# Four cross-attention and expert layers on one core: dense expert stages run by chunk with the next attention's opening inside, and other orders at the sparse stages

## The reference, cut to what matters

```python
# x: 2048 tokens x 256;  ctx: 1601 context rows x 192;  fp32 throughout
x = x + xattn(layernorm(x), ctx)    # L0: 16 heads of 16
x = x + ffn0(layernorm(x))
x = x + xattn(layernorm(x), ctx)    # L1: 16 heads of 16
x = x + ffn1(layernorm(x))
x = x + xattn(layernorm(x), ctx)    # L2: 8 heads of 32
x = x + ffn2(layernorm(x))
x = x + xattn(layernorm(x), ctx)    # L3: 16 heads of 16
x = x + ffn3(layernorm(x))

xattn:  q = x Wq + bq;  k = ctx Wk + bk;  v = ctx Wv + bv
        softmax(q k^T / sqrt(head)) v  Wo + bo
ffn0:   16 experts 256 -> 128 -> 256 with silu, 4 of 16 by sigmoid scores
        and groups, plus a shared silu layer 256 -> 512 -> 256
ffn1:   top 2 of 8 experts 256 -> 1024 -> 256 with gelu and biases
ffn2:   top 2 of 8 linear experts 256 -> 256 with biases
ffn3:   top 2 of 16 gated experts 256 -> 352 -> 256, at most 320 tokens
        each, plus a shared gated layer of the same size
```

## Time and profile before

| | |
|---|---|
| median of three runs | 3974.86 us (3974.20 to 3976.17) |
| the profiled execution | 3966.67 us |
| its span on the core | 3964.9 us |
| attention 0 and the routing of stage 0 | 0 to 775.0 us |
| dense stage 0, its first to its last matmul | 775.0 to 1069.5 us |
| last matmul of stage 0 to the first score of attention 1 | 78.9 us |
| sparse stage 1, first routed projection | 1827.87 us |
| dense stage 2, its first to its last matmul | 2859.9 to 2973.0 us |
| last matmul of stage 2 to the first score of attention 3 | 76.1 us |
| sparse stage 3, first routed transposes | 3739.41 us |

### The profile page before, as it was taken

How to read it: one execution, slowest core, us unless ns; L and a number is a source line. 1 busy time by engine, 2 the same in 40 slices (tenths; PEclk the granted TensorE clock), 3 DMA queues, 4 the chain that set the end, 5 groups by cost and what they waited for, 6 DMA issues and landing times. The chain is left out here.

```text
span 3964.9 us, 51571 instructions
## 1 busy us (share of the span) xinstructions
PE 3634.5 (92%) x17554; PEld 1586.3 (40%) x17555; DVE 2535.3 (64%) x5339; ACT 1936.7 (49%) x2351; POOL 689.4 (17%) x976
## 2 busy tenths in 40 slices
PE   5999999799889999977998599999797999998997
PEld 2333333456533333324665233332442333332564
DVE  5888887544588888834223555554467888885523
ACT  2677777412237777752333144444203777777111
POOL 4300000300130010014221401010403000001143
PEclk8999999899989999988999699999798999999998
DMA  7100000320010000025002300000411000001134
GB/s 137 41 18 18 14 18 6 68 43 19 15 45 18 17 14 18 9 68 192 30 30 59 100 18 18 17 18 6 86 20 49 18 14 18 17 11 44 40 125 137
DMA packets 132064, 163.82 MB, mean 41 GB/s; under 512 B 38315, under 2 KB 111645, under 8 KB 129681
## 3 DMA queue, kind: packets, MB, share of 16 engines
q1 hardware_dynamic: 121712, 135.08, 12.0%
q0 software_dynamic: 10144, 26.08, 3.4%
HBM read 123.93 MB, written 40.84 MB: 42 GB/s over the span
## 5 line engine op out<-in xcount | busy, mean ns | idle before, releaser
L1372 DVE TENSOR_REDUCE mx<-ps 128x1 f32<-128x400 f32 (+1 forms) x3584 | 1814.5, 566 | 434.2 <-PE ps L2019 422.5
L1101 ACT ACTIVATE probs<-ps,zero_col 128x1024 f32<-128x1024 f32 (+1 forms) x1040 | 1111.1, 1111 | 577.3 <-PE ps L2048 577.2
L2019 PE MATMUL ps<-k_stack,q_stack 97*128 97x400 bf16 (+1 forms) x3584 | 1089.4, 341 | 69.2 <-issue 27.6
L2048 PE MATMUL ps<-q_stack,k_stack 100*128 100x512 bf16 (+2 forms) x3328 | 1055.4, 381 | 5.4 <-ACT probs L1101 5.4
L2062 PE MATMUL ps<-probs,v 128*32 128x512 f32 (+2 forms) x5824 | 890.9, 607 | 0.2 <-ACT probs L1101 0.2
L2019 PEld LDWEIGHTS ps<-k_stack,q_stack 97*128 97x128 bf16 x3584 | 291.4, 97 | 1057.8 <-DVE mx L1372 663.1
L1101 ACT ACTIVATE probs<-ps,mask_col 128x1024 f32<-128x1024 f32 (+1 forms) x416 | 439.8, 1110 | 153.6 <-PE ps L2048 153.6
L2048 PEld LDWEIGHTS ps<-q_stack,k_stack 100*128 100x128 bf16 (+2 forms) x3328 | 324.1, 100 | 346.7 <-ACT probs L1101 63.2
L1479 DVE SCALAR_TENSOR_TENSOR x_res<-ps,comb,x_res 128x256 f32<-128x256 f32 x336 | 148.9, 483 | 155.1 <-PE ps L2267 155.0
L2062 PEld LDWEIGHTS ps<-probs,v 128*32 128x32 f32 (+2 forms) x5824 | 140.1, 111 | 258.4 <-issue 252.9
L872 POOL TENSOR_TENSOR o_t<-o_sum,recip_wide 128x512 f32<-128x512 f32 x32 | 40.8, 1274 | 738.7 <-DMA recip_wide<-row_recips 738.7
(11 more groups left out here) (285 smaller groups left out, 2851.2 us busy)
## 6 DMA issues: line engine op xcount, KB each, us to landing
q_stack<-q_parts SPq DMA_DIRECT2D x384, 64.0 KB, 2.3
q_parts<-qk_part SPq DMA_DIRECT2D x32, 384.0 KB, 2.5
w_up<-in_up SPq DMA_DIRECT2D x17, 704.0 KB
k_stack<-k_parts SPq DMA_DIRECT2D x48, 200.1 KB, 10.3
k_stack<-k_parts POOLq DMA_DIRECT2D x48, 200.1 KB, 18.1
k_parts<-qk_part SPq DMA_DIRECT2D x24, 384.0 KB, 2.9
w_all<-in_up SPq DMA_DIRECT2D x8, 1024.0 KB, 12.2
w_all<-in_down SPq DMA_DIRECT2D x8, 1024.0 KB, 12.7
```

Source lines behind the costliest of these rows:

```text
L1101: act.activation(PR[pair[0] % 4][0:r, :, :], PS[0:r, 2 * b:2 * b + 2, :], ACT.Exp, bias=mask_col[0:r, k:k + 1] if L == 3 else zero_col[0:r ...
L1372: ins = dve.reduce_max(MX4[g % 2][:, u, c:c + 1], PS[:, bank, 0:CK[c]], AX.X)
L2019: last = mm(PS[:, bank, 0:CK[c]], QS[g][0:97, slot_of(j), qt * P:(qt + 1) * P], KS[0:97, (g * hpg + j) * nsub, CKO[c]:CKO[c] + CK[c]], sta ...
L2048: last = mm(PS[0:r, b + i, :], KS[0:rows, (g * hpg + jj) * nsub + sub, k * P:k * P + r], QS[g][0:rows, slot_of(jj) + sub, :], start=sub == ...
```

## The change

**Dense stages.** The fences after stages 0 and 2 go. Both stages are written out unit by unit (`dense_units`): in stage 0 all 20 experts for chunk 0, then each expert for chunks 1 to 3; in stage 2 the 4 pairs for tiles 0 to 7, then for tiles 8 to 15. So chunk 0 of X is final after unit 19 (stage 0) or 31, of whose tiles the first four are final after unit 27. The weights are loaded twice, through a ring of 4 (one load per expert, up and down matrices merged) or 2. The shared slices come first. Down results have 3 banks (2 to 4), up results 2, pairs 4, since the side jobs' banks 5 to 7 are now in use.

**The opening inside.** `early_jobs` says at which unit each step of the next attention's opening is put: statistics of chunk 0, normalising, turning, queries, splits, and the 88 maxima and the turn, two jobs per unit in stage 0 from unit 33 and three in stage 2 from unit 30. SP stores and loads the first queries behind weight load 27 (stage 0) or 7 (stage 2) in its list (`queries`), and the max rows of group 0 behind load 39 or 8. Turning and querying chunks 1 to 3 become side jobs of group 0 of the first pass ("xturn", "xquery"); POOL normalises and splits chunk by chunk there.

**Sparse stage 1, entry.** VectorE doesn't wait for the biases before it reads the logits. `tokens_of_places` comes before `tiles_of_experts` and the weights, `tokens_at_places` on TensorE before the wait for the last key, and the bias matmuls behind the arrival of the first rows. POOL splits key parts 6 and 7 behind the first two gathers. **Exit:** SP loads all 16 tiles of answers before the keys. **Sparse stage 3:** `tokens_at_places` and `tokens_of_places` come one chunk earlier, the weights behind them.

```diff
+AHEAD = (1, 3)
+    if g == 0 and first and queries:
+        for d in range(1, NQ):
+            slots[3 * d] += [("xturn", d, 0), ("xturn", d, 1)]
+            slots[3 * d + 1].append(("xquery", d, 0))
+            slots[3 * d + 2].append(("xquery", d, 1))
+def dense_units(L):
+    if L == 0:
+        return [(e, c) for chunks in ([0], [1, 2, 3]) for e in range(20) for c in chunks]
+    return [(i, t) for tiles in (range(TPQ), range(TPQ, NT)) for i in range(4) for t in tiles]
+def early_jobs(L, hpg):
+    at = {0: dict(aggr=20, root=21, norm=22, turn=24, query=26, split=28, first=33, per=2),
+          2: dict(aggr=16, root=17, norm=18, turn=20, query=22, split=25, first=30, per=3)}[L]
...
@@ SP
-                    for par in range(2):
-                        load_expert(par, par)
+                    ring, queries, rows, loads = (4, 27, 39, 40) if L == 0 else (2, 7, 8, 8)
+                    for n in range(ring):
+                        load_matrices(n)
                     next_keys()
-                    with sp.Fori(1, items // 2) as i:
...
+                    for n in range(ring, queries):
+                        load_matrices(n)
+                    first_queries(L + 1)
+                    for n in range(queries, rows):
+                        load_matrices(n)
+                    store_max_rows(L + 1, 0)
+                    for n in range(rows, loads):
+                        load_matrices(n)
...
-                    for t in range(RING):
+                    for t in range(NT):
+                        if t >= RING:
+                            sp.wait_ge(s_ix, ix0[L] + 2 * (t - RING + 1))
                         load_answers(t)
                     load_constant_rows(2)
                     for g in range(NG):
                         load_keys(sp, 2, g)
-                    for t in range(RING, NT):
-                        sp.wait_ge(s_ix, ix0[L] + 2 * (t - RING + 1))
-                        load_answers(t)
...
-                fence(sp, fences)
+                if L not in (0, 2):
+                    fence(sp, fences)
@@ VectorE
-                dve.wait_ge(s_gl, gl.at())
+                if L != 1:
+                    dve.wait_ge(s_gl, gl.at())
...
+                        tokens_of_places()
                         tiles_of_experts()
-                        tokens_of_places()
+                        weight(0)
+                        weight(1)
+                        dve.sem_inc(s_wt, 1)
...
+                    for n in range(units):
+                        if L == 2:
+                            add_pair(n)
+                        early[2](slots.get(n, []), 0)
+                        if L == 0 and n > 0:
+                            add_unit(n - 1)
+                        early_part(at, n)
@@ TensorE
+                def down_unit(n, lag):
+                    load = n if n < 20 else 20 + (n - 20) // 3
+                    pe.wait_ge(s_hr, hr.at(lag))
+                    for i in range(TPQ):
+                        pe.wait_ge(s_yf, yf.at(2))
+                        yf.step()
+                        mm(PS[:, 2 + yj[0] % 3, 0:D], HTS[n % 2][:, 0, i * P:(i + 1) * P], weight_slot(load)[1],
+                           start=True, stop=True).then_inc(s_y, 1)
+                        yj[0] += 1
...
+                    for n in range(len(dense_units(L))):
+                        if L == 0:
+                            up_unit(n)
+                        else:
+                            pair_unit(n)
+                        if n == at["turn"]:
+                            turn_chunk(5, lambda i: XNC[:, i, :])
+                        if n == at["query"]:
+                            first_queries()
+                        if n == at["first"]:
+                            begin_maxima(L + 1)
+                        for job in slots.get(n, []):
+                            early[1](job)
+                        if L == 0 and n > 0:
+                            down_unit(n - 1, 1)
...
                 if L < 3:
                     project_next(L + 1, 0, positions if L == 1 else None)
+                    if L == 1:
+                        tokens_at_places(7)
                     pe.wait_ge(s_kc, kc.at())
...
-                        if L == 3 and c == NQ:
-                            pe.wait_ge(s_hr, hr.at())
-                            tokens_at_places(0)
+                        if L == 3 and c == NQ - 1:
+                            pe.wait_ge(s_yf, yf.at())
+                            tokens_at_places(7)
```

More of the change, by code:

```diff
@@ L944, in _ @@
                     gather_tile(1)
+                    for u in range(6, 8):
+                        split_keys(u, staged.take("key")[0])
                     for j in range(2, TILES):
@@ L1074, in _ @@
                     copy_projections(0, 1)
-                for d in range(1, NQ):
+                if L in AHEAD:
+                    xt.step(NQ - 1)
+                    for m in range(6):
+                        staged.take("query")
+                for d in range(1, NQ) if L not in AHEAD else []:
                     xt.step()
@@ new lines, in _, with routed @@
+                    dn.step(NT)
+                    def routed(par):
+                        tr.step()
+                        act.wait_ge(s_tr, tr.at())
+                        act.activation(XT[par][:], PS[:, 6:8, 0:CAP], ACT.Copy).then_inc(s_te, 1)
+                        for rows in ft:
+                            silu_unit(rows, CAP)
+                    loops = ((h, 2 * len(ft)), (hr, 2 * len(ft)), (tr, 2))
+                    with act.Fori(0, 8) as i:
+                        for c, per in loops:
+                            c.loop(i, 0, per)
+                        routed(0)
+                        routed(1)
+                        for c, per in loops:
+                            c.end(8)
@@ new lines, in pair_unit @@
+                def pair_unit(n):
+                    i, t = dense_units(2)[n]
+                    if t in (0, TPQ):
+                        load = i if t == 0 else 4 + i
+                        w[load % 2].step(16)
+                        pe.wait_ge(s_w[load % 2], w[load % 2].at())
+                    pe.wait_ge(s_yf, yf.at(6))
+                    yf.step(2)
+                    for k in range(2):
+                        last = mm(PS[:, n % 4, :], xnT[:, k, t * P:(t + 1) * P],
+                                  WUS[i % 2][:, k * 512:(k + 1) * 512], start=k == 0, stop=k == 1)
+                    last.then_inc(s_y, 1)
@@ new lines, in answer @@
+                    def answer(par):
+                        pe.wait_ge(s_hr, hr.at())
+                        for t in range(CT):
+                            r = P if t < CT - 1 else CLAST
+                            if yc.n > 1:
+                                pe.wait_ge(s_yc, yc.at(1 if t else 0))
+                            yc.step()
+                            for q, rows in enumerate(ft):
+                                last = mm(PS[0:r, 4 + t % 2, 0:D], HT[par][0:rows, q, t * P:t * P + r],
+                                          WD[1 - par][0:rows, q, :], start=q == 0, stop=q == len(ft) - 1)
+                            last.then_inc(s_y, 1)
@@ new lines, in _ @@
+                    rows_in(0)
+                    hidden(0)
+                    rows_in(1)
+                    answer(0)
+                    hidden(1)
+                    with pe.Fori(1, 8) as i:
+                        loops = [(hr, 2 * len(ft)), (w[0], nw), (w[1], nw), (xe[0], 16 * CT), (xe[1], 16 * CT),
+                                 (te, 2), (yc, 2 * CT)]
+                        for c, p in loops:
+                            c.loop(i, 1, p)
+                        for par in range(2):
+                            rows_in(par)
+                            answer(1 - par)
+                            hidden(par)
+                        for c, p in loops:
+                            c.end(7)
```

796 lines of the change are left out of this document (427 added, 369 removed).

## The result

The changed kernel takes 3905.82 us in the median of four runs (3900.06 to 3913.67), the kernel before 3974.53 (3969.91 to 3976.17): a ratio of 0.983, 95% interval 0.981 to 0.9851. The forecast was 3914, its range 3874 to 3946. The profiled execution took 3900.06 us, its span is 3898.4.

The account below looks back on a forecast made before the run. TensorE, busy 92% of the span, was taken as the bound, so only its idle, slow or added work counts. Terms -16.8 - 9.2 - 13.5 - 14.5 - 7.2 = -61.2 us gave 3905.5 profiled, 3914 median, range 3874 to 3946.

Parts of the forecast that it names:

- (b): Dense stage 0: fourth down matmul waits for its answer bank, 0.48 us in 45 units, 0.1 in 35 others.
- (f): First pass of attention 1: turning and querying chunks 1 to 3 moves into group 0, 13.0 us plus 1 for chains.
- (a): Dense stage 0: the opening's own TensorE work, 88 maxima, four query matmuls and eight transposes, 19.2 us.
- (c): Dense stage 0: TensorE's waits for weights while POOL's keys load, 15 us with the clock, bounds 0 and 28.
- (d): Dense stage 0: two query splits on VectorE and ACT's change to the root's table, 3 us, an estimate.
- (e): End of dense stage 0: waits for all adds and ACT's table loads, 7 us until TensorE is in step.
- Queues in turn: Dense stages: by the skill's rule weights pass between POOL's keys, the 15 + 8 us become nearly 0, sum 3891.
- Weights in turn: Rival for the dense stages: weights come in turn with the keys and TensorE stays fed, 3891 us; chance 0.12.
- openings for nothing: Rival: openings are hidden but cost what they save, only the sparse edits stay, 3940 us; chance 0.10.
- No bank wait: Rival for dense stage 0: answers' bank wait does not appear since maxima start sooner, 3892 us; chance 0.12.
- Starvation: Rival: weights wait wholly for keys in both dense stages, first query store at the exit too, 3939 us; chance 0.10.
- Lockstep: Rival: TensorE and VectorE take turns in dense units with maxima, +93 us, 4007 us; chance 0.05.

Follow-up runs that it names:

- adds-first run: Changed kernel with VectorE's adds before maxima in dense stage 0 and first queries before weight load 6 in stage 2: 3882.84 us, ratio 0.9793.
- keys-later run: Changed kernel with key loads held back, in dense stage 0 behind unit 16, in stage 2 groups 2 and 3 behind unit 12: 3870.12 us, ratio 0.9756.
- the last run: Changed kernel with both query projections of a chunk in one key tile of the first pass instead of two: 3898.28 us, ratio 0.9825.

## Why the prediction was right, point by point

The direction, the size and the places were right: -66.5 where -61.2 was summed up. Several terms missed, and in part against each other: (b) and VectorE's bound in stage 2 were 18 us too dear, the weights of both stages and (f) in both attentions 20 us too cheap. That the sum came within 5.3 us is in part luck.

*Dense stage 0.* (a) The opening's own work was right: 0.172 us a maximum, 0.86 a projection step. (b) The bank wait was right in kind and too large: 0.34 in 43 units, 14.6 us, where I had 0.48 in 45 and 0.1 in 35, 25.1 in all. The step that failed is the length of the two reductions: the first starts 0.38 behind the first maximum's matmul (923.64 to 924.02), as I said, but the two take 0.97 from start to next start, not 1.07 (0.10 of the 0.14); and units without maxima last 3.44, with nothing to add. The adds-first run shows the mechanism. (c) Weights cost 22.1 us, 15 was taken, 28 was the bound: the step that failed is sharing. 15 lay between even sharing and none; the keys moved five bytes for each of the weights'. The keys-later run shows that it is all theirs. In the other executions with the keys at their place the weights cost 20.8 to 26.8 us, so that the bound of 28 was nearly reached. The remaining terms, (d), (e) and the small waits, came to about 9 us where 10 was taken.

*Queues in turn.* The wait was 22.1 us, and 22.3 went when the keys were held back. The rule of the Trainium skill, page "DMA: Bandwidth & Descriptors", section "Queues, rings and completion order", that each DMA engine takes its queues in turn, a packet at a time, would by my reading have made (c) nearly nothing; that time was wrong here. The share of the queues does not say in which order single packets went, so only my reading's result is refuted: beside a queue that had up to 24 transfers to do, a weight load took 16.6 us for 2.6. Part of it is the size of the packets, which my reading left out: the keys' 4.08 MB went in 956 packets, 4.3 KB each, the weights' 0.82 MB in 449, 1.8 KB each. One for one, an estimate from these sizes, the weights would have had 30% of the bytes; they had 17%. The rest stays open.

*(f), first pass,* was too small in both attentions: 17.4 and 16.8 where 14 less 2 was taken. The term left out is what a projection pays for standing between scores; the last run shows that it is paid once per group of projections. Whether it is the change from bf16 to fp32 or another difference between the two was not tested. A key tile with a projection costs 2.12 more, not 1.72, and one with the turning 1.23, not 0.88: 3 x (1.23 + 2 x 2.12) = 16.4. The 2 us for the clock were not there in attention 1 (its first two scores took 1.06 as in the earlier trace rows) and were in attention 3 (0.60). The max rows came in time, as forecast.

*Dense stage 2.* VectorE is the bound, as forecast, but at 2.36 and 2.81 a unit, not 2.62 and 3.05: 22 x 0.64 + 8 x 1.09 = 22.8 us instead of 30.5. I had added whole durations (1.57 and 1.00) and a gap; from start to start three reductions take 1.44 and two adds 0.91. Weights came to 10.3 us in this execution (7.55 and the half clock) for 8, the queries' wait to 5.09 and 2 for 6.5; the 10 us of a store behind a 512 KB load were 9.84. For the queries' own work, the turn and the end of the stage 6.8 us are left of 160.2, where 9.9 was taken.

*Entry of sparse stage 1.* -15.1 for -13.5. The logits' step was 9.9 when the wait was put back and 9.1 alone on the kernel before, for 8.9. New is a wait ahead of the first projection: TensorE stands 1.69 us for SP's signal that the first expert's weights are there, which I had not seen.

*Exit.* -17.4 for -14.5: SP ends the fence, as forecast, but issues its 24 key loads in 14.0 us, not 17. The rival's late first query store did not come: store to first maximum took 7.3 us.

*Sparse stage 3.* The gap went, -5.8, confirmed by +6.1 when undone. The other 2.3 us can't be credited: the stretch behind it lasted 191.3 us here and 193.0 to 194.9 in the other runs with the same code. The half clock behind the gap was gone here and in two of those runs (6.5 us from the first routed product to the next transposes, 8.8 before), and there in four (8.0 to 8.2), though the gap was closed in all.

*The rivals.* Weights in turn and openings for nothing fell by stages 0 and 2. No bank wait fell by the adds-first run. Starvation was nearer than its 0.10 said for stage 0 (22 of 28), not for its other two places. Lockstep fell: VectorE idles 1.41 us in a unit of stage 0, and the unit lasts 4.12, not the 4.8 that lockstep needed.

## What to carry to other kernels

When bulk loads for the next stage stand on another queue, hold them back until the current stage's urgent loads are in; that alone was worth 34.8 us of TensorE's stretches here, and about 30 us of the whole by the ratios (0.983 to 0.9756). When work is interleaved on VectorE, let it first do what frees TensorE's next bank, and cost it from start to start, not by durations. Work moved out of an opening into a stretch where TensorE is never idle is paid there: count both stretches before calling it a gain. A wait that is removed pays only as far as what is late next: measure the stretch, as in the entry of sparse stage 1, where the key chain hung on the same step.

## What the runs showed of the hardware that was not expected

A 256 KB load took 2.6 us alone and 16.6 us beside 24 loads of 200 KB on the other queue, which took 4.08 of the 4.93 MB moved in that stretch, in packets of 4.3 KB against 1.8. fp32 matmul steps of 512 columns cost 0.86 us among their like, but 0.94 next to bf16 scores, with another 0.2 us before the first. A store and reload of queries took 9.84 us to its first use behind a 512 KB load on its queue and 7.41 to 7.42 without one.
